# Rank matmuls in one sweep, key stores behind the loads, and the last pair of chunks as two groups, in a two-layer cross-attention and mixture-of-experts kernel

## What is computed

```python
x = x + tanh(g_xattn[0]) * L0_xattn(layernorm(x), ctx, ...)   # additive pooling attention, 16 heads of 8
x = x + tanh(g_ffn[0])   * L0_ffn(layernorm(x), ...)          # 8 experts, 2 per token, relu
x = x + tanh(g_xattn[1]) * L1_xattn(layernorm(x), ctx, mask, ...)  # softmax attention, 16 heads of 8
x = x + tanh(g_ffn[1])   * L1_ffn(layernorm(x), ...)          # 2 of 8 experts per token, rows sorted by expert, gelu
```

## Time and profile before

| | |
|---|---|
| median of 3 runs | 910.71 us (910.56 to 911.73) |
| profiled execution | 904.8 us |
| its span, first to last instruction | 903.0 us |
| mean granted TensorE clock, share of full | 0.749 |
| PE busy | 531.1 us (59%), 4815 matmul records |
| DVE busy | 458.2 us (51%) |
| POOL busy | 385.7 us (43%) |
| ACT busy | 265.8 us (29%) |
| chain that ended last | DVE 25%, PE 25%, issue 16%, POOL 10%, DMA 8%, SP's queue 7%, unknown 7%, ACT 3% |
| PE busy, tenths in 40 slices | 2588683423288988880655575564552003999980 |

### The profile page before, as it was taken

One profiled execution on the slowest core, in us unless ns is written; L12 is line 12 of the kernel. 1 busy time (PEld: TensorE's weight loads), 2 busy tenths in 40 slices (PEclk: granted clock), 3 DMA queues, 4 the chain that ended last, 5 costly groups with the idle time before them and its releaser, 6 DMA issues.

```text
span 903.0 us, 16363 instructions
## 1 busy us (share of the span) xinstructions
PE 531.1 (59%) x4815; PEld 432.6 (48%) x4816; DVE 458.2 (51%) x1520; ACT 265.8 (29%) x442; POOL 385.7 (43%) x436
## 2 busy tenths in 40 slices
PE   2588683423288988880655575564552003999980
PEld 1256572310177877770433464443442002988870
DVE  4773696647022322337944678777685600322224
ACT  1220011102133433436211575373652101232220
POOL 5111116665145555553000353184666570655660
PEclk9886876655599999995655587585755555999995
DMA  7999999133243222213362543332104112322218
GB/s 197 262 166 190 176 170 168 58 83 92 68 105 85 75 67 64 65 43 110 116 199 73 135 105 92 89 115 55 37 25 127 38 47 63 80 73 70 74 48 282
DMA packets 108712, 94.56 MB, mean 105 GB/s; under 512 B 12344, under 2 KB 97080, under 8 KB 108584
## 3 DMA queue, kind: packets, MB, share of 16 engines
q1 hardware_dynamic: 94584, 70.04, 35.8%
q0 software_dynamic: 9840, 21.60, 8.2%
q10 hardware_dynamic: 4224, 2.10, 0.8%
HBM read 46.15 MB, written 47.45 MB: 104 GB/s over the span
## 4 chain that ended last, share of the span: by engine, by line
DVE 25%; PE 25%; issue 16%; POOL 10%; DMA 8%; SPq 7%; another core or an unknown queue 7%; ACT 3%; DVEq 0%; POOLq 0%; ACTq 0%
PE PS L701 22%; POOL ys L472 6%; DVE work L1208 3%; DMA work<-ys 3%; DVE XN L1231 3%; DVE stats L1213 2%; DVE work L1617 2%; DVE X L1208 2%; SPq L530 2%; POOL xs L461 2%; DVE rtmp L1208 2%; DMA q_parts<-w1l 1%; SPq L515 1%; DVE nwt L1224 1%
## 5 line engine op out<-in xcount | busy, mean ns | idle before, releaser
L701 PE MATMUL PS<-work 128*128 128x36 f16 (+6 forms) x1376 | 108.2, 258 | 95.8 <-DVE work L1208 70.6
L472 POOL DMA_INDIRECT ys<-work x144 | 141.1, 980 | 34.1 <-issue 34.1
L701 PE MATMUL PS<-w,work 128*128 x1152 | 144.6, 279 | 12.7 <-issue 6.3
L701 PEld LDWEIGHTS PS<-w,work 128*128 128x128 f32 x1152 | 134.9, 193 | 22.1 <-issue 20.8
L701 PEld LDWEIGHTS PS<-work 128*128 128x128 f16 (+3 forms) x1376 | 86.7, 137 | 118.6 <-issue 80.3
L497 POOL TENSOR_TENSOR work<-XN,work 128x1024 f16<-128x1024 f32 x32 | 68.1, 2128 | 162.8 <-ACT work L1152 162.5
L1208 DVE TENSOR_TENSOR work<-PS,work 128x128 f32<-128x128 f32 (+4 forms) x130 | 51.0, 414 | 153.3 <-issue 84.1
L461 POOL DMA_INDIRECT xs<-pack,adr_i x96 | 94.3, 983 | 66.8 <-ACT pack L1056 36.7
L701 PE MATMUL PS<-work,w1h 128*128 128x256 f16 x576 | 102.0, 278 | 8.6 <-DVE work L1519 7.2
L1104 ACT ACTIVATE work<-PS,b 128x256 f32<-128x256 f32 x160 | 62.7, 476 | 120.1 <-PE PS L701 105.3
L701 PE MATMUL PS<-work,w1l 128*128 128x256 f16 x288 | 80.1, 278 | 0.2 <-issue 0.2
(11 more groups left out here) (238 smaller groups left out, 837.9 us busy)
## 6 DMA issues: line engine op xcount, KB each, us to landing
xs<-zrow SPq DMA_DIRECT2D x8, 2210.0 KB
work<-xs SPq DMA_DIRECT2D x144, 65.0 KB
work<-ys SPq DMA_DIRECT2D x16, 512.0 KB, 4.4
k_parts<-work SPq DMA_DIRECT2D x24, 128.0 KB
q_parts<-w1l SPq DMA_DIRECT2D x24, 128.0 KB
w<-k_parts SPq DMA_DIRECT2D x8, 384.0 KB
work<-q_parts SPq DMA_DIRECT2D x8, 384.0 KB
work<-k_parts SPq DMA_DIRECT2D x32, 96.0 KB
```

The lines of the kernel that those rows point to most:

```text
L472: g.indirect_dma_start(ys[l], bass.IndirectOffsetOnAxis(xin[:, q, u, :].bitcast(U32)[:, D:D + 1], 0), yrow[:, q, u, :], None).then_inc(ff[ ...
L701: return t.matmul(o, lhsT, rhs, start=start, stop=stop, skip_group_check=True)
```

## The change

- `route_rank` takes all n tiles of a group at once: one matmul of the all-ones matrix by `cum16` broadcast over n tiles, then for each distance `back` one matmul of the all-ones matrix by the first n - back tiles into the last n - back, and one of the triangle by all: 9 matmuls for eight tiles, 5 for four. It holds for both layers.
- The stores of key parts 4 to 7 move behind SP's loop of expert loads.
- The low part of the values is subtracted at the head of DVE's step 4k-1 rather than near the end of step 4k-2.
- In the second layer the last pair becomes two groups of one chunk (five groups in all), and the steps of each group are a table. In a step DVE now does rows and packs ahead of `norm_scale`, choice and normalized rows.

Against the steps before, group 2 is chosen in 29 as before but normalized in 29 (30), ranked and read in 30 (31), packed in 30 and 31 (31 and 32). `RANK0`, the PSUM bank, POOL's program and its order of scatters stay; a scatter waits for its group's ranks.

```diff
@@ -341,6 +341,15 @@
+        def group(l, p):
+            return pair(p) if l == 0 or p < NP - 1 else tiles(p + NP - 1)
+
+        def group_of(l, c):
+            return c // 2 if l == 0 or c < NC - 2 else c - NP + 1
+
+        def width(t):
+            return t.stop - t.start
+
         def pack_of(l, c):
@@ -392,9 +401,14 @@
-        def pair_at(g, lead):
-            k, rest = divmod(g - lead, 2 * CT_TILES)
-            return k if rest == 0 and 0 <= k < NP else None
+        GROUPS = (NP, NP + 1)
+        ROUTE = {"norm": (12, 20, 28, 32, 36), "choose": (13, 21, 28, 33, 37), "normed": (14, 22, 29, 34, 37),
+                 "exp": (14, 22, 29, 34, 38), "rank": (15, 23, 30, 33, 37), "rows": (15, 23, 30, 35, 38),
+                 "pack": (15, 16, 23, 24, 30, 31, 36, 38), "high": (15, 15, 23, 23, 30, 31, 34, 38),
+                 "copy": (16, 17, 24, 25, 31, 32, 36, 39)}
+
+        def route_at(step, g):
+            return [k for k, at_ in enumerate(ROUTE[step]) if at_ == g]
@@ -454,7 +468,7 @@
             def scatter(l, c, parts=range(CT_TILES)):
-                pool.wait_ge(rt[l]["ranked"], c // 2 + 1)
+                pool.wait_ge(rt[l]["ranked"], group_of(l, c) + 1)
@@ -581,12 +595,12 @@
                     step(0, q)
+                with sp.Fori(1, rounds[l]) as i:
+                    for q in range(XS_LEAD):
+                        step(i, q)
                 if l == 0:
...
                         keys_stored(c)
-                with sp.Fori(1, rounds[l]) as i:
-                    for q in range(XS_LEAD):
-                        step(i, q)
                 for q in range(XS_LEAD):
@@ -805,17 +819,15 @@
                     pe.wait_ge(rt[l]["count"], p)
-                t0 = pair(p).start
-                for s in range(2 * CT_TILES):
-                    o = PS[:, BANK_RANK[l], RANK0 + s * E:RANK0 + (s + 1) * E]
-                    mm(o, ones16[:], cum16[:], stop=False)
-                    for b in range(s):
-                        mm(o, ones16[:], sel16[:, t0 + b, :], start=False, stop=False)
-                    ins = mm(o, tri16[:], sel16[:, t0 + s, :], start=False)
-                ins.then_inc(rt[l]["rank"], 1)
+                sel, n = sel16[:, group(l, p), :], width(group(l, p))
+                o = PS[:, BANK_RANK[l], RANK0:RANK0 + n * E].rearrange("p (s e) -> p s e", e=E)
+                mm(o, ones16[:], bc(cum16[:], 1, n), stop=False)
+                for back in range(1, n):
+                    mm(o[:, back:n, :], ones16[:], sel[:, 0:n - back, :], start=False, stop=False)
+                mm(o, tri16[:], sel, start=False).then_inc(rt[l]["rank"], 1)
...
             def route_total(l):
-                pe.wait_ge(rt[l]["count"], NP)
+                pe.wait_ge(rt[l]["count"], GROUPS[l])
                 mm(PS[:, BANK_RANK[l], TOTAL0:TOTAL0 + E], ones16[:], cum16[:]).then_inc(rt[l]["rank"], 1)
@@ -1022,8 +1034,7 @@
                     ins.then_inc(v9_ps, 1)
-                k = pair_at(g, 15)
-                if k is not None:
+                for k in route_at("rank", g):
                     pe.wait_ge(v9_lo, min(2 * k + 5, NC))
@@ -1057,7 +1068,7 @@
             def route_exp(l, p):
-                a.activation(wexp[:, pair(p)], wdif[:, pair(p)], ACT.Exp).then_inc(gap_exp, 1)
+                a.activation(wexp[:, group(l, p)], wdif[:, group(l, p)], ACT.Exp).then_inc(gap_exp, 1)
@@ -1178,16 +1189,12 @@
                     ins.then_inc(v9_sb, 1)
-                k = pair_at(g, 14)
-                if k is not None:
+                for k in route_at("exp", g):
                     route_exp(1, k)
-                for half in range(2):
-                    k = pair_at(g, 15)
-                    if k is not None:
-                        route_high(1, 2 * k + half)
-                    k = pair_at(g, 16 + half)
-                    if k is not None:
-                        route_copy(1, 2 * k + half)
+                for c in route_at("high", g):
+                    route_high(1, c)
+                for c in route_at("copy", g):
+                    route_copy(1, c)
             experts(1)
@@ -1349,21 +1356,22 @@
             def route_rows_normed(l, p):
+                t = group(l, p)
...
-                    dve.wait_ge(pack_hi, NC + 2 * (p - 1))
-                norm_rows(pair(p), slots(l, 2 * p).start, rt[l]["xn"])
+                    dve.wait_ge(pack_hi, NC + t.stop // CT_TILES - 4)
+                norm_rows(t, slots(l, t.start // CT_TILES).start, rt[l]["xn"])
...
             def route_lg(l, p):
-                t = pair(p)
+                t = group(l, p)
...
-                    link(tt(lg[:, t, :], lg[:, t, :], bc(brb[:], 1, 2 * CT_TILES), ALU.add))
+                    link(tt(lg[:, t, :], lg[:, t, :], bc(brb[:], 1, width(t)), ALU.add))
...
             def route_choose(l, p):
-                t = pair(p)
+                t = group(l, p)
...
-                a_, b_ = rtmp[:, 0, :, :], rtmp[:, 1, :, :]
-                rv = bc(rev[:], 1, 2 * CT_TILES)
+                a_, b_ = rtmp[:, 0, 0:width(t), :], rtmp[:, 1, 0:width(t), :]
+                rv = bc(rev[:], 1, width(t))
...
@@ -1380,12 +1388,12 @@
             def route_rows(l, p):
-                t = pair(p)
-                a_, b2 = rtmp[:, 0, :, :], rtmp[:, 1:3, :, :]
+                t = group(l, p)
+                a_, b2 = rtmp[:, 0, 0:width(t), :], rtmp[:, 1:3, 0:width(t), :]
...
-                tt(a_, PS[:, BANK_RANK[l], RANK0:RANK0 + 2 * CT_TILES * E].rearrange("p (s e) -> p s e", e=E),
-                   bc(expert_row[:], 1, 2 * CT_TILES), ALU.add).then_inc(rt[l]["rank_read"], 1)
+                tt(a_, PS[:, BANK_RANK[l], RANK0:RANK0 + width(t) * E].rearrange("p (s e) -> p s e", e=E),
+                   bc(expert_row[:], 1, width(t)), ALU.add).then_inc(rt[l]["rank_read"], 1)
...
@@ -1414,7 +1422,7 @@
             def route_table(l):
-                dve.wait_ge(rt[l]["rank"], NP + 1)
+                dve.wait_ge(rt[l]["rank"], GROUPS[l] + 1)
@@ -1594,6 +1602,14 @@
             for g in range(G0, G1):
+                k = chunk_at(g, -1)
+                if k is not None:
+                    dve.wait_ge(v9_sb, k + 1)
+                    for hb in range(2):
+                        ph = slice(hb * 64, hb * 64 + 64)
+                        v9 = [v[ph, k % 2, :, :, hb, 0:DH].rearrange("p s h d -> p (s h) d") for v in (v9h, v9l)]
+                        ins = tt(v9[1], PS[ph, 7, :].rearrange("p (n d) -> p n d", d=DH), v9[0], ALU.subtract)
+                    ins.then_inc(v9_lo, 1)
                 T = g - 5
@@ -1625,33 +1641,19 @@
                         tt(nmax16[:, 1, :], nmax, nmax16[:, 0, :], ALU.subtract).then_inc(n_ready, 1)
-                k = chunk_at(g, -2)
-                if k is not None:
-                    dve.wait_ge(v9_sb, k + 1)
-                    for hb in range(2):
-                        ph = slice(hb * 64, hb * 64 + 64)
-                        v9 = [v[ph, k % 2, :, :, hb, 0:DH].rearrange("p s h d -> p (s h) d") for v in (v9h, v9l)]
-                        ins = tt(v9[1], PS[ph, 7, :].rearrange("p (n d) -> p n d", d=DH), v9[0], ALU.subtract)
-                    ins.then_inc(v9_lo, 1)
-                k = pair_at(g, 12)
-                if k is not None:
-                    dve.wait_ge(x3_done, 2 * CT_TILES * (k + 1))
-                    norm_scale(pair(k))
-                    route_lg(1, k)
-                k = pair_at(g, 13)
-                if k is not None:
-                    route_choose(1, k)
-                k = pair_at(g, 14)
-                if k is not None:
-                    route_rows_normed(1, k)
-                k = pair_at(g, 15)
-                if k is not None:
+                for k in route_at("rows", g):
                     route_rows(1, k)
                     route_weights(1, k)
-                    route_pack(1, 2 * k)
-                k = pair_at(g, 16)
-                if k is not None:
-                    route_pack(1, 2 * k + 1)
+                for c in route_at("pack", g):
+                    route_pack(1, c)
+                for k in route_at("norm", g):
+                    dve.wait_ge(x3_done, group(1, k).stop)
+                    norm_scale(group(1, k))
+                    route_lg(1, k)
+                for k in route_at("choose", g):
+                    route_choose(1, k)
+                for k in route_at("normed", g):
+                    route_rows_normed(1, k)
                 k = chunk_at(g, 3)
```

## The result

The kernel after takes 901.0 us (median of four runs, 899.1 to 903.2) beside 911.2 of the kernel before in the same group of runs: a ratio of 0.9888, 95% interval 0.9857 to 0.9918. So it is faster by about 10 us, not by 35, and outside the range. I read stages from all of them.

The account below looks back on a forecast made before the run. It took rank-matmul waits in layer one, POOL's stores in the experts, and DVE then POOL's scatters in layer two as bounds. 19.5 + 0 + 15.5 = 35.0 off 910.7 gave about 876, range 866 to 886 (8 in 10: 860 to 897).

Parts of the forecast that it names:

- a stock of ready instructions, and what comes behind it trickles: Layer-one routing: TensorE runs the first 28 or so sel16 matmuls at full pace; the rest crawl, 0.94 us each.
- The larger term is the crawl ... so I let the waits go: Layer-one routing: nine matmuls end VectorE's rank waits, and POOL's 18.1 us idle between scatters goes; 19.5 us saved.
- Rival A: Waits beside scatters stay, from something else such as POOL's scatters holding up semaphores: 898, or 888 if partly healed; chance 0.19.
- Late key stores: Layer-one expert loads: 3 us won at the ninth tile's rows, 5.4 lost if tiles pair; taken as 0.
- The bound of -20: Low end for the moved key stores: layer one's tiles never paired after tile 14, 17 us, and 3 us.
- Rival B: Layer one's expert tiles behind the fourteenth stay single: 17 us more saved, 859; chance 0.12.
- Late value subtraction: Second-layer attention, steps 14 and 22: normalized rows fill DVE's wait for ScalarE; 4.3 us saved.
- Nine ranks in attention: Second-layer attention, pairs at steps 15 and 23: DVE's wait for rank matmuls shrinks; 2 us saved.
- I take 0.5: Second-layer attention: pair 2's rows ahead of the last scores delay the last value conversion by 0.5 us, at most 2.2.
- The split's tail: Second layer's last scatters: POOL's idle 5.5 and 7.0 us go, less 2.8 for slips.
- Rival D: Second layer: chunk 7 comes late by more than 7 us, DVE being held in step 31: 882; chance 0.05.

Follow-up runs that it names:

- e_ranks: Kernel before with the nine rank matmuls alone, where before takes 916.5 us: 906.8 us, ratio 0.9909.
- b_before: Kernel before, unchanged, run and profiled again: 918.2 us, ratio 1.0006.
- c_keys: Kernel before with the late key stores alone, where before takes 910.0 us: ratio 0.9984.
- c_nosplit: Kernel after with the second layer's routing in four pairs at the old steps, where before takes 910.0 us: 891.7 us, ratio 0.9807.
- a_v9: Kernel before with the late value subtraction alone, where before takes 861.9 us: ratio 0.9964.
- d_v9: Kernel before with the late value subtraction alone, again, where before takes 866.8 us: ratio 0.9951.
- b_hold: Kernel after with chunk 5 packed in step 32 instead of 31, where before takes 917.4 us: 894.6 us, ratio 0.9747.
- c_hold: Kernel after with chunk 5 packed in step 32 instead of 31, again, where before takes 910.0 us: 891.3 us, ratio 0.9825.
- groups 1 and 2: Two sets of experiments on the same chip, each sharing its runs of the kernel before: 861.9 us in the first, 917.4 us in the second.
- b_pause: Kernel after with POOL resting some 3 us after each chunk of 8 scatters in layer one: 911.1 us, ratio 0.9931.
- e_beforepause: Kernel before with POOL resting some 3 us after each chunk of 8 scatters in layer one: 918.0 us, ratio 1.0014.

## Why the prediction was wrong

It was right about the sign, about where the kernel waits, and in that the matmuls crawl beside POOL's scatters and not before them. Its picture of "a stock of ready instructions, and what comes behind it trickles" fits the pattern; that the stock is one of fetched instructions isn't shown. It was wrong about the size, at two steps: layer one was forecast at 19.5 us and moved its first expert load by 5.1, layer two at 15.5 and gained 0.1 to 0.5.

*"The larger term is the crawl ... so I let the waits go": 19.5 us of layer one.* This step failed. What starves isn't TensorE alone: VectorE crawls too, and SyncE's tail stores are slower. I took VectorE's and ScalarE's chain (choose, weights, rows, addresses, copy) as ready to run at its normal pace once the matmuls were short; it stalls within the same run of scatters. So POOL's idle time between groups fell from 18.1 to 11.4 us, the first load came 5.1 us earlier, and the nine matmuls alone gave 0.9% (`e_ranks`, 8 us). The row that could have told me was there: the earlier trace rows has POOL waiting for VectorE's addresses and ScalarE's copy, beside scatters each time, and I looked only at the matmuls ahead of them.

*Rival A* said that the waits stay and gave 898, or 888 if they heal in part, with 0.19 together. Its cause, something in POOL's scatters, is the one that came, and the matmuls' crawl has the same cause. That 898 lies so near 901 is luck: it had 1.5 us for layer one and 11.3 for layer two, where the traces have 5 and less than 1. By the Trainium skill ("Runtime: NRT & Kernel Launch", "Instruction fetch mechanics") fetching is mostly hidden. The traces don't speak against it: no block for TensorE is on its way during the crawl in `b_before`, and in `before` and `c_keys` none arrives between 148 and 192 either.

*Late key stores, 0 us.* Right where it was forecast (0.9984), and for the reason given: in `after` and `c_keys` the stall before the ninth tile is gone and the tiles go in pairs nearly throughout. The bound of -20 was never near there; in the other condition the part is the largest single one, 6.5 us. Rival B's state, tiles one by one, is that of the 862 condition, and there they are the faster ones, 142 us for 40 where pairs take 162 to 164.

*Late value subtraction, 4.3 us.* Right in size. From the first to the last value conversion it takes 177.4 us before, 177.3 with the nine matmuls alone and 173.2 in `c_nosplit`: 4.1. In the other condition it gives 3 and 4 us by itself (`a_v9`, `d_v9`).

*Nine ranks in attention, 2 us.* Nothing up to the last conversion: 177.4 and 177.3.

*The split, "I take 0.5" for the rows ahead of the last scores.* Mis-sized. In the trace after, the same stretch is 177.3 again: steps up to 28 keep the 4 us won, and the last three take 21.0 us where `c_nosplit` has 18.0, and what moved there is pair 2's routing, which now stands in VectorE's queue in front of what TensorE needs. At 862 it is 176.0 against 169.6 us.

*The split's tail, 5.5 + 7.0 - 2.8.* Failed. 5.5 us of idle time came down to 3.3, but 7.0 became 9.4: the hold of step 31, which I had bounded at 5 us and given no price, was 8.93, and put tile 29's normalization, chunk 6's ranks and its copy beside chunk 4's and 5's unbroken scatters, where they stall until 707.6. Rival D named this hold, though with layer one's gain intact. `b_hold` undoes it and has 10 us back in its group. With four pairs the tail takes 56.9 us from last conversion to the first read behind the scatters, before and after 59.7, in `c_hold` 53.8; of the 3.1 us that the better placing wins there 1.9 are lost in the attention ahead of it.

Together, for the 910 condition: 8 (ranks) + 1 (keys) + 4 (subtraction) + some 4 that no single part shows = 17 to 18 for `c_nosplit`, less 5 to 7 for the split as written, makes the 10 measured. The intervals of `c_nosplit` and of the kernel after overlap in part, so by the ratios the 5 to 7 have an uncertainty of about as much; the stage has them more closely, 237.0 less 230.1 = 6.9 us. Of the 4 that no part shows it has up to 2.8, in the tail (59.7 to 56.9). I can't place the rest: layer one's experts, for one, take anything from 161.0 to 167.9 us in traces of kernels with early key stores.

**What stays open.** Why some groups of runs have the stalls and others not: the pace of scatters, and in groups 1 and 2 the chip, are the same, and I can't tell whether a queue, memory placement or something outside the core makes it. Nor what exactly is starved. The matmuls that wait for nothing look like a want of instructions, but the blocks of TensorE's queue don't bear that out; VectorE's pairs of independent steps, which come together while dependent ones stand 0.7 us apart, would fit a delay in what each step needs to be passed on. Whether the waits without a releaser in the experts have the same cause wasn't tried. The 4 us that no part shows weren't tried apart, and the subtraction alone was never run at 910.

## What to carry to other kernels

When one engine's work crawls beside another engine's unbroken run of indirect DMAs, ask which other engines work beside that run: shortening the work of the first victim hands the stall to the next, and what is gained is only the difference. Test the cause before costing the cure: keep the suspect, rest the engine next to it, and see whether the suspect runs at pace. And when work is moved forward in a queue written out by hand, look at what the wait in its first instruction holds behind it: one step later was worth 10 us here.

## What the runs showed of the hardware

- The same kernel took 862 to 867 us in two groups of runs and 910 to 917 in four, steady within each group; in the first, layer one's scatters followed one another without a wait in every trace, and 36 rank matmuls beside them took 1.0 to 1.2 us.
- In the slower condition TensorE and VectorE, some 8 to 14 scatters into a back-to-back run (one each 1.27 us), issued one step each 0.71 us, or at 1.42 and 2.13. SP's eight tail stores took 16 to 17.4 us in eight traces there, but 9.8 in `c_hold`, and 9.0 to 10.6 in the other condition.
- During the crawl of 167 to 179 us in `b_before` no block of instructions arrived in the queue that I take for TensorE's; the last one had come at 147.
- Behind 2 us without a scatter, in the middle of 16, VectorE showed no "remote" wait for the rest of the group in two of three cases; behind rests of 2.9 us after each 8 (`b_pause`, `e_beforepause`) POOL waited for nobody.
